# The first weight block's transfer split by partitions over the two hardware queues, ahead of the indices

## The reference

```python
def layer0(x, conditions, weights):
    w = weights[conditions]                       # (32, 64, 64)
    return jnp.einsum('bct,bcd->bdt', x, w)

def layer1(x, W, A, Bm, scalings, adapter_idx):
    H = jnp.einsum('btd,od->bto', x, W)
    xa = jnp.einsum('btd,brd->btr', x, A[adapter_idx])
    delta = jnp.einsum('btr,bor->bto', xa, Bm[adapter_idx])
    return H + delta * scalings[adapter_idx][:, None, None]

x = x + layer0(x, itok_B_1_198, L0_cond_weights)
x = x + layer1(x, L1_cond_W, L1_cond_A, L1_cond_Bm, L1_cond_scalings, itok_B_0_6)
```

## Time and profile before

| what | value |
|---|---|
| median of 3 runs | 77.64 us (77.55 to 78.07) |
| the profiled execution, its time | 77.68 us |
| its span, from the first to the last instruction | 76.0 us |
| PE busy | 71.5 us, 94% of the span |
| DVE, ACT, POOL busy | 55.2, 51.4 and 33.6 us |
| DMA | 14.55 MB, 190 GB/s over the span |
| chain that ended last, by engine | PE 71%, DMA 9%, DVE 5%, issue 5%, ACT 4% |

### The profile page before, as it was taken

The page is one execution under the profiler, slowest core; times in us unless marked ns, Lnnn a source line. Parts: engine busy times, 40 slices in busy tenths (PEclk is TensorE's granted clock), DMA queues, the critical chain, the costliest instruction groups (busy, mean ns, idle before and its releaser), DMA issues.

```text
span 76.0 us, 1936 instructions
## 1 busy us (share of the span) xinstructions
PE 71.5 (94%) x464; PEld 65.1 (86%) x464; DVE 55.2 (73%) x144; ACT 51.4 (68%) x126; POOL 33.6 (44%) x76
## 2 busy tenths in 40 slices
PE   3989999999999999999999999999999999999940
PEld 3957887785999699999999999999999999999930
DVE  4007954987979797979597968977797949675920
ACT  0725956995896597686768666968687767567440
POOL 5700591499799906354354515580655260000000
PEclk9999999999999999999999999999999999999999
DMA  0899479436789989578967963579416430303025
GB/s 0 208 417 390 118 213 236 142 113 205 234 284 281 306 276 294 210 243 225 302 207 214 311 220 70 151 201 312 156 39 237 138 138 4 138 13 138 0 97 179
DMA packets 9677, 14.55 MB, mean 191 GB/s; under 512 B 3650, under 2 KB 4418, under 8 KB 9666
## 3 DMA queue, kind: packets, MB, share of 16 engines
q1 hardware_dynamic: 7554, 9.16, 36.9%
q0 software_dynamic: 1536, 4.20, 18.4%
q10 hardware_dynamic: 576, 1.07, 4.5%
HBM read 10.23 MB, written 4.19 MB: 190 GB/s over the span
## 4 chain that ended last, share of the span: by engine, by line
PE 71%; DMA 9%; DVE 5%; issue 5%; ACT 4%; POOL 1%; POOLq 0%; ACTq 0%
PE z_ps L653 45%; PE z_ps L641 9%; DMA head<-head_a 5%; DMA b_raw<-b_t 4%; PE out_ps L708 4%; PE out_ps L709 3%; PE out_ps L695 3%; PE out_ps L713 3%; PE v_ps L687 2%; DVE b_stack L521 2%; DVE a_table L590 1%; ACT out_sb L413 1%; ACT a_table L427 1%; ACT x_high L387 1%; POOL b_raw L287 1%
## 5 line engine op out<-in xcount | busy, mean ns | idle before, releaser
L653 PE MATMUL z_ps<-moving,x_high 128*128 128x272 f32 x224 | 33.5, 290 | 0.0
L653 PEld LDWEIGHTS z_ps<-moving,x_high 128*128 128x128 f32 x224 | 29.9, 188 | 0.6
L287 POOL DMA_DIRECT2D b_raw<-b_t x32 | 16.1, 506 | 11.3 <-issue 5.2
L653 PE MATMUL z_ps<-moving,x_low 128*128 128x272 f32 x112 | 18.6, 288 | 0.0
L280 POOL CAST moving<-a_table 128x128 fp32r x28 | 9.1, 355 | 17.0 <-PE z_ps L653 14.3
L653 PEld LDWEIGHTS z_ps<-moving,x_low 128*128 128x128 f32 x112 | 15.8, 188 | 0.0
L512 DVE TENSOR_TENSOR z_low<-z_ps,z_high 128x272 fp32r<-128x272 f32 (+1 forms) x28 | 11.8, 422 | 1.4 <-ACT z_high L364 0.5
L521 DVE TENSOR_TENSOR b_stack<-b_raw,b_high 128x512 fp32r<-128x512 f32 x16 | 11.9, 741 | 0.2 <-ACT b_high L380 0.2
L380 ACT ACTIVATE b_high<-b_raw,group_sb 128x512 fp32r<-128x512 f32 x16 | 11.5, 716 | 0.2 <-DMA b_raw<-b_t 0.2
L364 ACT ACTIVATE z_high<-z_ps 128x272 fp32r<-128x272 f32 (+1 forms) x28 | 10.5, 376 | 0.2
L394 ACT ACTIVATE v_high<-v_ps,group_sb 128x128 fp32r<-128x128 f32 x16 | 5.8, 366 | 7.0 <-PE v_ps L687 6.9
(11 more groups left out here) (59 smaller groups left out, 76.6 us busy)
## 6 DMA issues: line engine op xcount, KB each, us to landing
b_raw<-b_t POOLq DMA_DIRECT2D x32, 128.0 KB, 3.2
out<-out_sb SPq DMA_DIRECT2D x15, 256.0 KB, 3.0
x_raw<-xt SPq DMA_DIRECT2D x13, 256.0 KB, 3.8
w_sb<-w SPq DMA_DIRECT2D x32, 16.0 KB, 3.1
w_late<-w_late_t SPq DMA_DIRECT2D x1, 480.0 KB, 6.9
head<-head_c ACTq DMA_DIRECT2D x1, 400.0 KB, 4.7
head<-head_d SPq DMA_DIRECT2D x1, 384.0 KB, 5.7
head<-head_a ACTq DMA_DIRECT2D x1, 264.0 KB, 3.5
```

Of the source, the lines that this page charges most:

```text
L287: pool.dma_start(b_raw[s * C:(s + 1) * C, t % BBUFS, :], b_t[ds(which[s], 1), :, :].rearrange("a r (g n) -> (a r) g n", g=1) .to_broadcast ...
L653: last = nc.tensor.matmul(z_bank(t, part), x[:, t % XBUFS, k * P:(k + 1) * P], moving[:, int(n == HL), k, at:at + HALF], start=((n, k) == ...
```

## The change

The transfer of `head_a` becomes two transfers of 64 partitions each. SP issues partitions 0 to 63, as its first transfer, ahead of the indices; ACT issues partitions 64 to 127, in the place where it issued the whole. Both count on the same semaphore, so the two engines that wait for it, ACT in `high_of_w` and PE ahead of its first product, wait for 32 in place of 16.

```diff
+            sync.dma_start(head[0:P // 2, HEAD_AT[0]:HEAD_AT[1]], head_a[0:P // 2, :]).then_inc(head_loaded[0], 16)
             sync.dma_start(index_sb[:], heads.rearrange("(a n) -> a n", a=1)).then_inc(index_loaded, 16)
             sync.dma_start(head[:, HEAD_AT[1]:HEAD_AT[2]], head_b).then_inc(head_loaded[1], 16)
             sync.dma_start(head[:, HEAD_AT[3]:HEAD_AT[4]], head_d).then_inc(head_loaded[3], 16)
...
-            act.dma_start(head[:, HEAD_AT[0]:HEAD_AT[1]], head_a).then_inc(head_loaded[0], 16)
+            act.dma_start(head[P // 2:P, HEAD_AT[0]:HEAD_AT[1]], head_a[P // 2:P, :]).then_inc(head_loaded[0], 16)
             act.dma_start(head[:, HEAD_AT[2]:HEAD_AT[3]], head_c).then_inc(head_loaded[2], 16)
...
                 if p < 2:
-                    act.wait_ge(head_loaded[0], 16)
+                    act.wait_ge(head_loaded[0], 32)
                     act.wait_ge(head_loaded[p + 1], 16)
...
-            pe.wait_ge(head_loaded[0], 16)
+            pe.wait_ge(head_loaded[0], 32)
             plain_products(0, W_PART, in_turn[:1])
```

## The result

The changed kernel takes 82.09 us (median of 4 runs, 81.12 to 82.26) against 77.68 us (77.55 to 78.07) of the kernel before: a ratio of 1.053, with a 95% interval from 1.044 to 1.062. The forecast was 78.0, within 77.3 to 78.9. It is slower by 4.4 us, over ten times what I had summed up. The profiled execution took 82.10 us with a span of 80.4, so again 1.7 us lie around the span, and the whole loss is inside.

The account below looks back on a forecast made before the run. PE was taken as the bound, passing on any shift at 9 us. The halves 0, SP's later transfers 0 and the late head_b +0.34 took 77.68 to 78.02, forecast as 78.0 us, range 77.3 to 78.9.

Parts of the forecast that it names:

- Where the kernel is bound: PE, busy in all of 45.81 us from 26.69 on; a shift of PE at 9 us is passed on.
- Part 1: head_a in two halves at the kernel's head: between 0.27 us gained and some 0.1 lost, taken as zero.
- the zero that I took for the landing: head_a's landing ahead of PE's first product: neither sooner nor later for being split, 0 us.
- Part 3: Head transfers: head_b, issued after head_c, lands at 6.0 in place of 5.0; PE's products end 0.34 us later.
- served whole, in the order in which they had been issued: DMA engines at the head finish each first transfer before the next; order becomes a, a, c, b.
- the term of +1.0 us for its landing: head_b lands behind head_c's 128 packets, 1.01 us over 16 engines: 6.0 in place of 5.0.
- The clock: Rival, chance 0.13: PE's idle 0.6 us or more delays the clock's rise; half the 14 passes slow gives +1.9, 79.6 us.
- the idle 0.27 us: PE's wait for head_a before 4.39 us; it did not prevent the clock's rise, taken as evidence against a clock loss.
- The warm-up work: TensorE's work ahead of its first products, read as some 4 us, after which they still ran at half speed.
- ACT's copy: take_z(0) ahead of tile 2, done at 8.58, read as 0.3 us before PE is free at 8.90.
- Part 2: SP's later transfers go out 0.39 us later; the gathers have over two us left, so covered; up to 0.4 otherwise.
- the late head_b: PE at the head waits for head_b till 6.02; 14 passes end at 9.24 against 8.90: +0.34 us.

Follow-up runs that it names:

- the spare load: The kernel before with the index transfer issued twice by SP, the first into a tile nobody reads: 78.42 us, ratio 1.010.
- the fillers: The changed kernel with 12 more products of ones on TensorE between t0k0 and the wait for head_b: 80.55 us, ratio 1.034.

## Why the prediction was wrong

**Where the kernel is bound** was right: one shift of PE ahead of 9 us is passed on, and it was (12.84 against 9.06, and 4.42 at the end).

**Part 1, the halves, failed in its second sentence**: "An issue takes 0.35 for the one-row index load and 0.38 for 128 partitions, so half the partitions save nothing." It is worse than nothing: 0.58, 0.57, 0.55 and 0.61 in the profiles above. With it head_b's issue began at 2.02, where I had 1.68, and the gathers' at 6.99, where I had 6.55. A hint stood in my own: four gathers of 64 partitions in 2.48 us, 0.47 to 0.53 for one issue. I had used that row for its start and not read its duration. No saving at PE's start is shown: with the halves on two queues the first product was at 4.03, 4.19, 4.24, 4.59 and 4.67 in five profiles, with head_a whole at 3.92, 3.92, 4.23 and 4.39 in four. So the zero that I took for the landing stands; it was what the longer issue did to the transfers behind that I had at nothing. The Trainium skill's "Don't bother" ("DMA: Bandwidth & Descriptors", "Rules for kernel authors"), which I had weighed as a zero, was right in its sign and too mild: no run here shows the two halves as merely equal to the whole.

**Part 3, the order on the wire.** That head_b would fall behind head_c was right, and the spare load shows the mechanism alone, with head_b at 5.59 where I had 6.02. What failed is "served whole, in the order in which they had been issued", at the pace read from the kernel before, taken over to a program with 64-partition transfers in front. There head_c and head_b went side by side at 205 GB/s in place of 405, and head_b landed at 7.71, not at 6.0: the term of +1.0 us for its landing was +2.7, and what PE made of it +2.2 in place of +0.34. The split by columns, with the same order, the same bytes and the same two queues, had 390 GB/s and head_b by 5.5. So it is the 64 partitions. By what path is less clear than these rows suggest: with the fillers head_c was served first, at 328 GB/s, and head_b was later still (8.3). What all six profiles with 64-partition halves share is a late end of the head's stream: w_late landed at 9.2 to 11.0, against 8.5 to 9.1 in the seven others. What in the engines makes them so was not shown.

**The clock** was the rival, at a chance of 0.13, and its condition was written down: idle time of over 0.6 us. I priced half of the passes slow at +1.6 on top of +0.34; it was +1.5 by the fillers and +1.6 by the rows. Its place and its price were right, its chance far too low; it came with a wait of 2.83 us and not of 0.6, so it is not the same case. I took the idle 0.27 us that did no harm as evidence that 0.6 would do little. In the split by columns 0.46 us sufficed in the run that was profiled, and the times of two more fit it; in the spare-load kernel 0.93 us did no harm in any of four runs, but the same head with tile 5's x moved had 7 of 12 at 79.0 us or more. The kernel before had none in 35 runs. It is a risk that idle time opens, not a fixed price. The changed kernel paid in another way. Its two passes of t0k0 lie 0.33 apart (0.72 - 0.39), less than the 0.46 of half speed, so the clock had risen by then, and behind the idle 2.83 us it was down again, which I had not considered. The fall is in all three profiles in which PE, its clock risen, then waited for over 2 us (2.83, 3.23 and 2.18; in the last it came at 7.7, after three passes at full speed), and not in the spare-load kernel, whose passes of t0k0 lay 0.37 apart (0.76 - 0.39) ahead of an idle 0.93.

Two readings of the prediction were off without a part in this. The warm-up work ahead of the first products lasted 2.93 us (from 1.20), not some 4. And tile 2's first product started at 8.69, not 8.90, so ACT's copy, done at 8.58, had 0.1 us to spare and not 0.3.

**Part 2, SP's later transfers**, "covered", was wrong too. No gather or x tile was late, as I had said, but the load of tile 2's B, on another queue, took 1 us longer with the spare load and 0.8 longer in the changed kernel. That is where the 0.6 or 0.7 us of the loss that comes after the head shows. Whether SP's push is its cause stays open: with the fillers, and SP pushed further, B took 3.21 us and no loss came after the head (2.75 at tile 2 and 2.8 in the span).

Terms of the sum, forecast and measured: head_a's halves 0 and 0; the late head_b +0.34 and +2.2; the clock 0 (as a rival +1.6) and +1.5 to +1.6; B's load 0 and +0.6.

## What to carry to other kernels

Read the duration of an issue from a row of the same shape, not of the nearest one; and once an issue grows, follow what stands behind it on its queue and on the other one. A chain at the head of a program has a second price, the clock: an idle stretch of TensorE of half a microsecond among its first products can cost 1.5 to 2 us, so a forecast should ask of each new wait there whether TensorE has something to do in it, and a few products of ones are a cover, itself not quite free. If a first transfer must be split over two queues, split its columns, not its partitions; but no split tried here beat the whole transfer.

## What the runs showed that I had not expected

- Half of head_a by partitions took 0.55 to 0.61 us to issue, the whole 0.38, half of it by columns 0.40 or 0.41; right behind two of the first kind, one on each queue, an issue of 128 partitions took 0.59 to 0.85, where the same ones took 0.37 to 0.46 before.
- The engines' rate from 3.4 to 5.0 us: 405 GB/s before, 380 with the spare load (358 with tile 5's x moved as well), 387 to 408 in the three kernels split by columns; 205, 254 and 328 in three profiles of the changed kernel's transfers, 277 with head_b and head_c exchanged, 331 with both halves on ACT, 331 with head_b ahead of the indices.
- TensorE's clock went up at 5.91 in the kernel before, and only at about 9.6 in the column split, where TensorE's work up to t1k0 differed only by a t0k0 that started 0.47 us sooner and 0.46 us of idle time behind it.
- The load of tile 2's B on POOL's queue took 3.13 us in the kernel before and 3.21 to 4.13 in nine of the others; what sets it was not found.
